# Attention kernel on one core: later weight loads, a later patch projection and the second tile's squares ahead of its rotation

## The reference, cut to what matters

```python
xn = _layernorm(x)
x = x + _L0_attn_ref(xn, Wqkv, Wout, bout) + _L0_ffn_ref(xn, wqkv, q_scale, k_scale, wo, ln_g, ln_b, w1, b1, w2, b2)
```

```python
dots = jnp.einsum('brhsd,brhtd->brhst', q, k) * scale
attn = jax.nn.softmax(dots, axis=-1)
out = jnp.einsum('brhst,brhtd->brhsd', attn, v)
```

```python
q = l2norm(q) * qs
k = l2norm(k) * ksc
q, k = rotary_xpos(q, k)
o = local_attention(q, k, v)
x = x + o.transpose(0, 2, 1, 3).reshape(b, n, INNER) @ wo
# then layer norm, h @ w1 + b1, a * gelu(g), h @ w2 + b2
```

## Time and profile before

| | |
|---|---|
| median of 3 runs | 389.63 us (387.52 to 389.82) |
| the profiled execution | 390.88 us |
| its span, first to last instruction | 389.1 us |
| PE, DVE, ACT, POOL busy | 90%, 69%, 75%, 66% of the span |
| mean granted PE clock | 0.98 |
| first patch scores, start | 13.54 us |
| first mask matmul of tile 0, start | 50.71 us |
| mask matmuls of tiles 1, 2 and 3 of the first layer, start | 58.64, 66.11 and 73.57 us |

### The profile page before, as it was taken

One profiled execution on the slowest core, in us unless ns is written; L12 is line 12 of the kernel. 1 busy time (PEld: TensorE's weight loads), 2 busy tenths in 40 slices (PEclk: granted clock), 3 DMA queues, 4 the chain that ended last, 5 costly groups with the idle time before them and its releaser, 6 DMA issues. The chain is left out here.

```text
span 389.1 us, 10787 instructions
## 1 busy us (share of the span) xinstructions
PE 348.4 (90%) x4007; PEld 265.4 (68%) x4007; DVE 267.7 (69%) x470; ACT 291.1 (75%) x887; POOL 257.9 (66%) x248
## 2 busy tenths in 40 slices
PE   1858779999999999988897869999999999988995
PEld 1646557888888888655454548888888888665562
DVE  4546767788878878466775676887888788365453
ACT  2556378999998999975467686899999989973620
POOL 2997479999999999720056588888998898410000
PEclk9998899999999999999999898999999999999998
DMA  6975032322322232215100122223222222200001
GB/s 192 363 153 182 3 123 56 76 56 62 72 62 49 62 77 56 49 36 182 50 0 0 28 55 47 52 63 77 55 65 62 68 58 63 60 12 7 27 27 54
DMA packets 35298, 27.63 MB, mean 71 GB/s; under 512 B 19077, under 2 KB 29231, under 8 KB 34735
## 3 DMA queue, kind: packets, MB, share of 16 engines
q1 hardware_dynamic: 34959, 26.49, 25.7%
q10 hardware_dynamic: 288, 0.46, 0.4%
HBM read 9.64 MB, written 1.05 MB: 27 GB/s over the span
## 5 line engine op out<-in xcount | busy, mean ns | idle before, releaser
L1111 ACT ACTIVATE probs<-ps,neg_max 128x128 f32<-128x128 f32 x256 | 90.0, 377 | 2.2 <-DVE neg_max L1316 1.2
L620 POOL TENSOR_TENSOR qkn<-work 128x512 f32<-128x512 f32 x64 | 80.6, 1282 | 15.4 <-DVE work L1272 5.5
L634 POOL TENSOR_TENSOR probs_n<-probs,row_inv 128x512 f32<-128x512 f32 x64 | 66.6, 1042 | 16.8 <-DVE row_inv L1321 14.6
L628 POOL TENSOR_TENSOR qkn<-qkn,rnorm 128x512 f32<-128x512 f32 x64 | 65.5, 1046 | 15.8 <-ACT rnorm L1067 15.1
L1111 ACT ACTIVATION_READ_ACCUMULATOR probs<-ps,neg_max 128x1 f32 x256 | 55.1, 215 | 0.0
L1060 ACT ACTIVATE work<-ps 128x1024 f32<-128x1024 f32 x32 | 32.8, 1026 | 22.0 <-issue 12.6
L1316 DVE TENSOR_REDUCE neg_max<-ps 128x4 f32<-128x512 f32 x64 | 41.0, 682 | 6.0 <-PE ps L834 6.0
L1262 DVE TENSOR_REDUCE ss_pair<-work 128x16 f32<-128x1024 f32 x32 | 39.0, 1220 | 8.0 <-ACT work L1060 6.1
L189 PE MATMUL ps<-wqkv_hi,h_hi 128*128 128x512 f32 x96 | 42.4, 442 | 1.6 <-ACT work L1060 1.6
L813 PE MATMUL ps<-small,qkn 128*128 128x128 f32 x256 | 37.1, 281 | 4.7 <-POOL qkn L628 4.6
L848 PE MATMUL ps<-small,probs_n 128*128 128x128 f32 x256 | 36.7, 282 | 5.1 <-POOL probs_n L634 2.8
(11 more groups left out here) (129 smaller groups left out, 758.3 us busy)
## 6 DMA issues: line engine op xcount, KB each, us to landing
v_off<-v_tok SPq DMA_DIRECT2D x64, 128.0 KB, 2.3
k_t<-k_t SPq DMA_DIRECT2D x30, 128.0 KB, 2.3
cos_w<-in_cos_t SPq DMA_DIRECT2D x2, 1024.0 KB, 8.0
sin_w<-in_sin_t SPq DMA_DIRECT2D x2, 1024.0 KB, 10.4
x_shift<-x SPq DMA_DIRECT2D x64, 32.0 KB, 1.9
x_raw<-in_x SPq DMA_DIRECT2D x4, 256.0 KB, 4.5
x<-xin SPq DMA_DIRECT2D x8, 128.0 KB, 5.5
out<-o_t SPq DMA_DIRECT2D x4, 256.0 KB, 2.3
```

The lines of the kernel that those rows point to most:

```text
L620: pool.tensor_tensor(to, first, second[:, :, ::-1, :], ALU.add).then_inc(rot_summed, 1)
L628: pool.tensor_tensor(of, of, rnorm[:, part * HEADS:(part + 1) * HEADS].unsqueeze(2) .broadcast_to([P, HEADS, DH]), ALU.mult).then_inc(rot_ ...
L634: pool.tensor_tensor(probs_n[:, 4 * g:4 * g + 4, :], probs[:, 4 * g:4 * g + 4, :], row_inv[:, 4 * g:4 * g + 4].unsqueeze(2).broadcast_to([ ...
L1111: e = act.activation(probs[:, k, :], s_ps[g][:, cw * P:(cw + 1) * P], ACT.Exp, bias=neg_max[:, k:k + 1], accum_out=row_sum[:, k:k + 1])
```

## The change

It has four parts.

1. **SP's list.** The loads of `wo`, `a_wout`, `w2` (three parts) and the vectors go from between the second and the third shifted input group to behind all four groups, `w1` and the second layer's `wqkv`.
2. **Patch steps.** The second chunk of patch queries and keys is projected in step 1, behind the values, and not in step 0; ACT takes it there too. The turns of input groups 2 and 3 and ACT's copies go from steps 2 and 3 to steps 3 and 4. ACT's roundings move: second half of `wqkv` from step 1 to 2, input groups to steps 2, 4, 5 and 6, masks from step 4 to 3, `w1` from step 6 to the tail step 7. POOL takes the remainder of input group 0 ahead of the sine table.
3. **Tile 1 in banks of its own.** Queries and keys of tile 1 go to banks 2 and 3, and are projected right behind those of tile 0. `project_v(0)`, which writes bank 2, now waits for `rot_done` 4, which is the second rotation of tile 1.
4. **Squares ahead of the rotation.** ACT squares tile 1 right behind tile 0 (`norms(1)`, once DVE has summed the squares of tile 0), DVE sums them behind those of tile 0, and rotates tile 1 only then.

```diff
-        qk_ps = bank(0, 2)
+        def qk_of(n):
+
+            return bank(2, 2) if n == 1 else bank(0, 2)
+
...
             shift_input(0)
             shift_input(1)
+            shift_input(2)
+            shift_input(3)
+            sp.wait_ge(xn_tr, SPANS)
+            sp.dma_start(w1_raw, w1.rearrange("l p n -> p l n")).then_inc(w1_in, 16)
+            sp.wait_ge(masks_done, 1)
+            sp.dma_start(wqkv_raw[1], wqkv[1]).then_inc(wqkv_in[1], 16)
             sp.dma_start(wo_s[:], wo.rearrange("l (c p) n -> p l c n", p=P)).then_inc(w_in, 16)
             sp.dma_start(a_wout_s[:], a_wout_t).then_inc(fw_in, 16)
...
             sp.dma_start(vectors[:], vectors_d).then_inc(fw_in, 16)
-            shift_input(2)
-            shift_input(3)
-            sp.wait_ge(xn_tr, SPANS)
-            sp.dma_start(w1_raw, w1.rearrange("l p n -> p l n")).then_inc(w1_in, 16)
-            sp.wait_ge(masks_done, 1)
-            sp.dma_start(wqkv_raw[1], wqkv[1]).then_inc(wqkv_in[1], 16)
...
             split_wqkv()
+            split_first(0)
             scale_table(sin_w, sin_in)
-            for g in range(SPANS):
+            for g in range(1, SPANS):
                 split_first(g)
...
             def project_qk(layer, n):
                 pe.wait_ge(h_split, split_before(n + 1))
-                after(pe, sq_done, n)
+                if n != 1:
+                    after(pe, sq_done, n)
...
-                if t in (2, 3):
-                    if t == 2:
-                        pe.wait_ge(a_qk_taken, 2)
-                    else:
-                        pe.wait_ge(xin0_done, 3)
-                    turn_input(t)
+                if t == 3:
+                    pe.wait_ge(a_qk_taken, 2)
+                    turn_input(2)
+                if t == 4:
+                    pe.wait_ge(xin0_done, 3)
+                    turn_input(3)
                 if there(t, A_STEPS):
                     project_patch_values(t)
-                if t == 0:
+                if t == 1:
                     project_patch_qk(1)
...
                     project_qk(0, 0)
+                    project_qk(0, 1)
 
             over_patches(pe, patch_step, in_front)
             turn_patch_out(0)
-            project_qk(0, 1)
             turn_patch_out(1)
...
                     after(pe, v_evac, n)
+                    if n == 0:
+                        pe.wait_ge(rot_done, 4)
...
-                if t == 0:
+                if t == 1:
                     take_patch_qk(1)
-                if t in (2, 3):
-                    take_input(t)
-                if t in (0, 1):
+                if t in (3, 4):
+                    take_input(t - 1)
+                if t in (0, 2):
                     if t == 0:
                         act.wait_ge(wqkv_in[0], 16)
-                    round_part(0, t * W_PART)
-                if t in (2, 3, 4, 5):
-                    round_first(t - 2)
-                if t == 4:
+                    round_part(0, t // 2 * W_PART)
+                if t in (2, 4, 5, 6):
+                    round_first((2, 4, 5, 6).index(t))
+                if t == 3:
...
-                if t == 6:
+                if t == A_STEPS:
                     act.wait_ge(w1_in, 16)
...
             def norms(n):
                 after(act, qk_ready, n + 1)
-                after(act, rot_done, 2 * n + 2)
-                after(act, ss_done, 2 * n)
-                act.activation(sq[:], qk_ps, ACT.Square).then_inc(sq_done, 1)
+                if n != 1:
+                    after(act, rot_done, 2 * n + 2)
+                after(act, ss_done, 2 * n - 1 if n == 1 else 2 * n)
+                act.activation(sq[:], qk_of(n), ACT.Square).then_inc(sq_done, 1)
...
             norms(0)
+            norms(1)
             inverse_norms(0)
...
-                    if there(t + 2) and (layer == 0 or t >= 0):
+                    if there(t + 2) and t >= 0:
                         norms(n + 2)
...
             def sum_squares(n):
                 after(dve, sq_done, n + 1)
+                if n == 1:
+                    dve.wait_ge(ss_done, 2)
...
                 after(dve, qk_ready, n + 1)
+                if n == 1:
+                    dve.wait_ge(sq_done, 2)
...
             sum_squares(0)
+            sum_squares(1)
             put_patches(0)
             rotate(1, 1, cos_w)
...
-                    if there(t + 2) and (layer == 0 or t >= 0):
+                    if there(t + 2) and t >= 0:
                         sum_squares(n + 2)
```

More of the change, by code:

```diff
@@ L691, in project_qk @@
                 pe.wait_ge(h_split, split_before(n + 1))
-                after(pe, sq_done, n)
+                if n != 1:
+                    after(pe, sq_done, n)
                 for part in range(2):
                     span = slice(part * INNER, (part + 1) * INNER)
-                    mm = matmul3(pe, qk_ps[:, span], input_tile(n),
+                    mm = matmul3(pe, qk_of(n)[:, span], input_tile(n),
                                  (wqkv_hi[:, layer, span], wqkv_lo[:, layer, span]))
@@ L1270, in rotate @@
                 after(dve, qk_ready, n + 1)
+                if n == 1:
+                    dve.wait_ge(sq_done, 2)
                 after(dve, rot_summed, 2 * n)
                 dve.tensor_tensor(to[:].rearrange("p (a h d) -> p a h d", a=2, d=DH),
-                                  qk_ps.rearrange("p (a h d) -> p a h d", a=2, d=DH),
+                                  qk_of(n).rearrange("p (a h d) -> p a h d", a=2, d=DH),
                                   table[:, t, :, :].unsqueeze(2).broadcast_to([P, 2, HEADS, DH]),
```

## The result

The changed kernel took 394.82 us (median of 4 runs, 394.63 to 395.48), the kernel before 389.73 beside it: ratio 1.0153, 95% interval 1.0115 to 1.019. Timed again with more runs (e13, 10 runs) it took 393.42 against 388.97: ratio 1.011, interval 1.0075 to 1.0145. It is slower by 1.1 to 1.5%, that is by 4.5 to 5.1 us; the forecast was +0.8 us (390.4), no change that could be told. The first median lies just outside the forecast's range of 387.0 to 394.4, the second inside it. The profiled execution has a span of 393.7 us against 389.1, so 4.6 us are to be found.

A forecast was written before the change was run, and what follows sets the result against it. The prediction took a chain of dependent steps, no engine's busy time, as the bound. Terms +0.35 - 4.85 + 5.3 - 1.0 + 1.0 gave +0.8 us, so 390.4 us, range 387.0 to 394.4.

The forecast's parts named there:

- The 4.85 us for the stop: Patch step 3: later loads remove PE's 3.07 us instruction stop and the slow clock behind it, gaining 4.85 us.
- The terms of parts 3 and 4: Seam around tiles 0 and 1: +5.3 us for the longer chain, -1.0 given back, +1.0 for the clock.
- the two large terms: The 4.85 us gain at the loads and the 5.3 us loss at the seam, expected to nearly cancel.
- the rule that tile 1 decides the end: Tile loop: what is early or late at tile 1's mask matmuls is early or late at the end.
- +0.35 was taken: Patch steps: step 2's scores start at 21.8 us, 0.35 later, with bounds of -0.15 to +1.8 us.
- POOL's list costs nothing: Patch steps: POOL gets `wqkv`'s second half about 1 us later, at no cost; without cover it would cost 1 us.
- The chain of T+13.25: Seam: `project_v(0)` starts 13.25 us behind the first tile projection (T), where it took 7.93: +5.3 us.
- the squares gave 0.92 back for 1.0: Seam: DVE's sum for tile 1 no longer stands before the first maxima, giving back 1.0 us.
- the clock took 0.71 for 1.0 before tile 0: Seam: PE's idle time may halve its clock, slowing transposes and scores; taken as +1.0 us, at most 2.3.
- my -1.4 to +3.5: Bounds of the summed change in time, in us, around the forecast of +0.8.
- The first rival: Patch step 3: PE's stop stays despite the later loads, so the kernel is slower, 395.3 us; chance 0.14.

The follow-up runs named there:

- e13: The changed kernel, unchanged, profiled and timed again: 393.42 us against 388.97, ratio 1.011.
- e1: The kernel before with only the six weight loads moved later: 386.37 us against 388.86, ratio 0.9941.
- e15: The kernel before, unchanged, profiled again: ratio 0.9998.
- e14: The changed kernel with five filling matmuls at the change of layers and none in the seam: 392.96 us, ratio 1.0097.
- e3: The kernel before with only the patch-step changes, second chunk projected in step 1 and roundings moved: 389.3 us against 388.86, ratio 1.002.
- e4: The kernel before with the later loads and the patch-step changes, old seam kept: 388.06 us against 388.86, ratio 0.9972.
- e5: The changed kernel with three filling matmuls on PE at the change of layers: 392.1 us, ratio 1.0084.
- e10: The changed kernel with tile 1 back in banks 0 and 1, its squares' sum again before the first maxima: 387.66 us, ratio 0.9956.
- e6: The changed kernel with seven filling matmuls in the seam, in front of `project_v(0)`: 392.61 us, ratio 1.0087.
- e9: The changed kernel with filling matmuls in all three gaps, seven in the seam and five at the change of layers: 390.56 us, ratio 1.0036.
- e11: The changed kernel with the rounding of `w1` back in patch step 6: 393.6 us, ratio 1.011.
- e7: The changed kernel with the second patch chunk projected and taken in step 0 as before: 392.81 us, ratio 1.0109.
- e8: The kernel before with the later loads and ACT's squares of tile 1 ahead of its rotation, old banks: 386.64 us, ratio 0.9933.
- e12: The kernel before with later loads, ACT's early squares in old banks and five filling matmuls at the layer change: 384.38 us against 389.19, ratio 0.9869.
- e2: The kernel before with only tile 1's own banks and the squares ahead of the rotation: 393.19 us against 388.86, ratio 1.0111.

## Why the prediction was wrong

**The steps that failed are two terms of the sum.** The 4.85 us for the stop came from one execution and were carried over to the median, where the later loads gave 2.5 us (e1). And the half clock behind the wait that part 2 puts in front of the weighed values had no term; it took 1.05 us of step 2 in the profile. With 2.5 in place of 4.85 and +1.05 for the clock the sum would have been +4.2 us; 4.5 to 5.1 were measured. The terms of parts 3 and 4, which make the loss, were nearly right, so the two large terms did not cancel as forecast. Besides, the rule that tile 1 decides the end did not hold.

**What bounds the kernel: right up to tile 1, wrong as a rule for the end.** The rule was "What is early or late at tile 1 is early or late at the end". In the two profiles tile 1 was 2.91 us late and the end 4.6; in e15 and before it was 2.15 us early and the end 0.6. Tiles 1 to 15 and 18 to 31 take the same time everywhere (within 0.3 and 0.2 us), but the way from 15 to 18 took 71.65 to 75.34 us by the clock that PE had there. The Trainium skill, page "TensorE: Matmul & The Clock Gate", Part 1, says of a kernel's start that the number of slow matmuls differs between runs of one kernel. The traces agree there: step 1's values took 1.91 us in the changed kernel and 1.04 in e14, whose code is the same up to there. The traces show the like at the change of layers (73.29 and 75.09 us for the kernel before), and differences of up to 3 us between kernels without filling there are as large as what was asked. The loss of 1.7 us there belongs to this pair of profiles: over both profiles of each kernel the way from 15 to 18 is 74.7 us changed and 74.2 before, while tile 1 is at 61.2 and 57.6. So most of the loss is in front of tile 1.

**Part 1, the stop: mechanism right, size wrong.** The later loads take the stop away (e1, and every run with them), the stop follows the instruction count, and its end follows the packet (e3). It remains an inference that the packet waited behind the loads inside the DMA engines; no row shows its queue. The Trainium skill, page "Runtime: NRT & Kernel Launch", section "Instruction fetch mechanics", says that crossing a block is mostly hidden. Here the measurement decides: behind the same 449 records PE stopped for 1.73 to 3.07 us in four profiles. In all four the DMA engines had been full or nearly so just before (share 0.91 to 1.15 in 22 to 24 us). The term was 4.85 us and should have been 2.2 to 4.6, by e1's time 2.5. That was the largest error against the median: I priced the stop from one execution which lay 1.25 us above its median, and set that difference aside.

**Part 2: at its bound, and a price not in the sum.** +0.35 was taken and +1.62 came, inside the bound of 1.8: the values and the first row of the chunk were slow. The wait that this makes, 2.09 us, is in the chain as ACT's copies. What had no term is the half clock behind it, 1.05 us in step 2. I had looked for the clock behind the stop and behind the seam, but not behind the wait that the change adds. This half clock doesn't always come. Of the nine profiles with the late chunk and the later loads, five have step 2 at 3.4 to 3.75 us (changed, e4, e5, e10, e13) and four at 2.67 to 2.68 (e6, e9, e11, e14). Their tile projections start at 35.05 to 37.56, against 34.84 to 35.05 in the four with the later loads and the early chunk (e1, e7, e8, e12). That POOL's list costs nothing held (e7 and e1 have the projection at the same time).

**Parts 3 and 4: right.** The chain of T+13.25 was 12.98 to 13.00 in every profile that has it unshortened, +5.05 for +5.3; the squares gave 0.92 back for 1.0; the clock took 0.71 for 1.0 before tile 0. Through tile 1 it cost more, 1.5 us in the changed kernel's profile and up to 2.8 in others (e6).

**Sum by the profile:** +1.62 - 3.55 + 5.05 + 0.71 - 0.92 = +2.91 at tile 1, within my -1.4 to +3.5, and +1.73 at the change of layers, outside of any term. Of the 3.8 us between the forecast's +0.8 and the profile, 1.3 are step 2's later start, 1.3 the smaller gain from there to the projection (1.05 of them the half clock), and 1.7 the change of layers; the seam was 0.5 cheaper. That the forecast's own bounds at tile 1 hold the +2.91 is partly luck: the profile of before was the one with the dearest stop; against e15's tile 1 the changed kernel is 5.1 us late. The first rival had the right sign and nearly the time (395.3), but not by its mechanism: the stop did not stay.

**Open:** whether the half clocks at the change of layers are tied to the changed front. 15-18 was 75.0 and 74.4 in the changed kernel and 73.3 and 75.1 in the one before; four profiles can't tell. Between e4 and the changed kernel lie 5.4 to 7.0 us of time, where the forecast's terms (5.3 - 1.35 for the `w1` rounding - 1.0 + 1.0) give 3.95. How much of the rest is the clock through tile 1, and how much the spread of the times, is not shown either.

## What to carry to other kernels

A result in a PSUM bank that the next step must write to puts its whole way out of the bank in front of that step: follow the bank's readers to the last, not only the engine's list, before an early projection is called free. Price a stop from several profiles, and give every new wait of PE of 2 us and more a term for the clock behind it. If the spread of one kernel is larger than the gain that is asked about, look for the stretch that makes the spread; here one stretch, the change of layers, differed by up to 3 us between kernels with the same code there.

## What the runs showed of the hardware

- PE stopped behind the same 449 matmul and weight-load records for 1.73, 2.25, 2.28 and 3.07 us, while the DMA engines carried a backlog of loads, and went on 2.4 to 2.6 us behind the start of an instruction packet each time. Moving 0.93 MB of loads behind that point removed the stop.
- After waits of 2 us and more PE's granted clock fell from the full to the half level in some profiles and not in others. Behind the same wait of 2.09 us it fell in the changed kernel and not in e3 and e14. Behind a stop it fell after 3.07 us (before) and 2.28 (e3), and not after 2.25 (e15) or 1.73 (e2).
- Matmuls whose result nobody reads kept the clock up: with five of them at the change of layers 15-18 took 71.65 us where the same kernel without them took 75.00, one profile each. In the times of the changed kernel they gave nothing that can be told (e14 against e13).
